# Wider contractions in the attention of an audio tower: 64 rows become 68 or 128, the added rows zero

## The chip, the cores and the metric

The kernel runs on one core of a Trainium2 chip, in one launch. The metric is the device time of that core in microseconds (us). The engines named below are TensorE (PE in the profile, its weight loads PEld), VectorE (DVE), ScalarE (ACT), GpSimd (POOL) and the queue engine SyncE (SP).

## The reference, cut to what matters

The input is x of shape (16, 750, 64). Three stages follow each other: a token stage (two dense layers, a square, two dense layers, a strided convolution that leaves 375 positions), a bidirectional recurrent stage over the 375 positions, and an attention whose keys and values are looked up with product keys. Only the last one is touched:

```
b, n, d = x.shape                                   # 16, 375, 64
q = (x @ Wq).reshape(b, n, HEADS, DIM) * DIM ** (-0.5)
kv_scores, indices = _pk(x, Wq_pk, pk_keys)         # 2 x top 16 of 64, then top 16 of the sums, softmax
ind = indices + offsets[None, None, :, None]
k = jnp.einsum('bnhk,bnhkd->bnhd', kv_scores, keys_table[ind])
v = jnp.einsum('bnhk,bnhkd->bnhd', kv_scores, values_table[ind])
sim = jnp.einsum('bihd,bjhd->bhij', q, k)
attn = jax.nn.softmax(jnp.where(causal, sim, neg), axis=-1)
out = jnp.einsum('bhij,bjhd->bhid', attn, v)
out = out.transpose(0, 2, 1, 3).reshape(b, n, HEADS * DIM)
return out @ Wo
```

There are 8 heads of 64 elements, so the scores, the queries, q times k, and v times Wo all contract over 64 elements.

## The kernel before, in words

The function `attention` works through 16 batches of 375 positions, cut in three pieces of 125. For heads 0 to 3 the table rows are gathered by GpSimd's indirect DMAs into `rows` and summed by TensorE with the weights `wmat` (the unit "eat"). For heads 4 to 7 the whole table of a head is multiplied: a batch has 64 steps (`STEPS`), and each step p has a fixed part on every engine.

- TensorE: `exponent` for step p+1 (products `ps<-parts,half`, and at each eighth step also `ps<-kdup,u`, which contract over 68 rows), `product` for step p-1 (`ps<-w,dtab`, 375 columns in 32 bits, contracting over 128 rows), `ranks` for step p+1 (`ps<-rank,half`, bf16), then the small units placed in this step.
- ScalarE: the exponential `ex` of the step, and copies out of PSUM for the units.
- VectorE: `weight`, which makes `w` from the rank sums and `ex`, then slices of the top-16 search for the next batch ("front").

Each product in 32 bits is two matmul records in the trace, each with its own weight load; the trace names it by weights and moving operand in alphabetical order.

The small units that contract over 64 rows are these, per batch: 24 `sim` (`ps<-kvT,qt`, q times k, 125 to 375 columns), 8 `value` (`ps<-cst,kvT`, three products of 64 columns each, v times Wo, on rows 64 to 127), 4 `query` (`ps<-u_dense,cst`), 8 `part` (`ps<-u_dense,kpart` or `ps<-u_front,kpart`), 3 `score` and 3 `score2` (`ps<-keymat,u_front`, 512 columns), and one opening of the output sum (in `weigh`, `ps<-cst` and `ps<-cst,h_now`). That is 51 units. Everything else that TensorE does in a batch contracts over 68, 125 or 128 rows.

In a step TensorE takes the units of bank 5, then of bank 6, then `weigh`, then the front's. `places()` puts the units into steps by fixed tables (`SIM_AT`, `PART_AT`, `VALUE_AT`, `QUERY_AT`) and a running sum of VectorE's time. By it part 0 of the next batch stands in step 49, and the unit "turn" that brings the max rows of the second piece into `u_front[64:68]` in step 44. Two of the 64-row units follow each other directly in five places per batch (steps 4, 11, 14, 25, 39), so a batch has 46 separate excursions to 64 rows. Before the first batch a prologue (`front` alone for 64 steps) does the search for batch 0; after the last one an epilogue finishes the last heads.

TensorE begins the attention with waits on the table `half`, which GpSimd's queue loads, and on the keys placed by VectorE.

Of the kernel before, what the change touches and what calls it, by code (L numbers as in the profile page):

```python
# [10 lines left out]
F32 = mybir.dt.float32  # L11
# [29 lines left out]
GH = 4  # L41
# [42 lines left out]
def build(nc, x, pack, early, halves, table, dense, minus, out):  # L84
    hu = nc.dram_tensor("rows_in", (2, B, D, T), F32).ap()
    with ExitStack() as ctx:
        cst = ctx.enter_context(nc.sbuf_tensor("cst", [128, WIDTH], F32))
        keymat = ctx.enter_context(nc.sbuf_tensor("keymat", [64, 1024], F32))
# [383 lines left out]
def turn_and_fold(nc, col, states, hist, keymat, ps):  # L472

    with nc.semaphore("b_key_product") as s_mm, nc.semaphore("b_copied") as s_cp, nc.Block() as block:
# [7 lines left out]
        @block.scalar  # L482
        def _(act):
            nc.scalar.copy(hist[0:64], states[:, :, 0:B]).then_inc(s_cp, 1)
            act.wait_ge(s_mm, 1)
            nc.scalar.copy(keymat[:].rearrange("p (k n) -> p k n", k=4), ps[0:64, 0:4, 0:256]).then_inc(s_cp, 1)
            act.wait_ge(s_cp, 3)
# [229 lines left out]
def attention(nc, cst, keymat, halves, table, dense, minus, hu, out, ps):  # L717
# [10 lines left out]
    with ExitStack() as ctx:  # L728
# [15 lines left out]
        kpart = sb("kpart", [64, DH, 2, 4, NK // 2])  # L744
# [7 lines left out]
        h_now = sb("h_now", [64, T])  # L752
# [25 lines left out]
        qt = sb("qt", [64, H, T])  # L778
# [11 lines left out]
        s_kdup = sem("d_keys_placed")  # L790
# [74 lines left out]
        def _(sp):  # L865
# [12 lines left out]
            def batch(n, kind):  # L878
                sp.wait_ge(s_cur, n + 1)
                sp.dma_start(h_now[:], hu[0, bass.ds(n, 1)].rearrange("o d t -> (o d) t")).then_inc(s_h, 16)  # L880
# [22 lines left out]
        def _(pool):  # L903
            pool.dma_start(half[:], halves[:]).then_inc(s_half, 16)
# [15 lines left out]
        def _(pe):  # L920
# [5 lines left out]
            pe.wait_ge(s_kdup, 16 + 4)  # L926

# [4 lines left out]
            def front(p, kind, b, f0):  # L932
                n = b - 1
                for which in range(2):
                    for key in here(which, p, kind):
                        name, c = key
                        f = f0 + c
                        if name == "score":
                            free(0, kind, n, key)
                            pe.wait_ge(s_row, b * 16 + 16)  # L940
                            mm(ps[0:TT, 5, :], u_front[0:64, c * TT:(c + 1) * TT], keymat[:, 0:512]).then_inc(s_fs, 1)
                        if name == "score2":
                            free(1, kind, n, key)
                            pe.wait_ge(s_row, b * 16 + 16)
                            mm(ps[0:TT, 6, :], u_front[0:64, c * TT:(c + 1) * TT], keymat[:, 512:1024]).then_inc(s_fs2, 1)
# [95 lines left out]

            def sim(m, kind, n):
# [3 lines left out]
                mm(ps[0:TT, 5, 0:(c + 1) * TT], qt[:, h, c * TT:(c + 1) * TT], kvT[0:64, h, 0:(c + 1) * TT]).then_inc(s_s, 1)  # L1046
# [9 lines left out]
            def weigh(m, kind, n):  # L1056
# [4 lines left out]
                if m == OLD:  # L1061
# [3 lines left out]
                    mm(ps[0:TT, 7, 0:NT * D], cst["causal"][0:64, 0:TT], cst["wq"][0:64, 0:NT * D], start=True, stop=False)  # L1065
# [587 lines left out]
```

## Time and profile before

| | us |
|---|---|
| median of 3 runs | 7148.5 |
| lowest and highest | 7143.23 and 7180.57 |
| the profiled execution | 7117.53 |
| its span | 7115.6 |

The profile is of one execution on the core. Its span covers the first to the last instruction, and 1.9 us lie around it. The profiled execution is 31 us (0.4%) below the median of the runs. The span has three parts: the token and recurrent stages (to 1027 us), the prologue of the attention (1027 to 1245 us), and its 16 batches with the epilogue (from 1245 us). A busy TensorE is not a TensorE at its peak: matmuls are pipelined and each record covers the way through the array too, so times between starts tell more than durations. TensorE's clock is granted at one of two levels, 1.2 and 2.4 GHz; a mean of 1.00 is 2.4 GHz throughout and 0.50 is 1.2 GHz throughout.

### The profile page before, as it was taken

Reading aid. Unit: us, or ns where it says so; the run is one execution under the profiler, and the core shown is the slowest. Engines: PE = TensorE matmul, PEld = TensorE weight load, DVE = VectorE, ACT = ScalarE, POOL = GpSimd, SP = SyncE. Lnnn points to the kernel's source line nnn. Section 1 sums busy time; section 2 is a strip of 40 time slices with the busy share of each in tenths; the row PEclk is TensorE's granted clock in tenths of the full one; section 3 lists DMA queues with packets and bytes.
Section 4 is the critical chain, followed back from the end, with each engine's and each line's share of the span. In section 5 each row is a group of like instructions: output and inputs, shape, how many; then the busy total and the mean of one; then the engine's idle time right before and its main releaser. Section 6 shows DMA issues by size and latency. Waiting matters only on the chain.

```text
span 7115.6 us, 93479 instructions
## 1 busy us (share of the span) xinstructions
PE 5480.1 (77%) x24308; PEld 3418.3 (48%) x24308; DVE 4305.4 (61%) x16637; ACT 2239.6 (31%) x5719; POOL 3127.9 (44%) x3404
## 2 busy tenths in 40 slices
PE   5666650778787888878888787878787888787889
PEld 4444420445454555545555454545445545454556
DVE  4666657666666565757566666665656575656522
ACT  4333320233332333333333232323333333333323
POOL 0011103555545455555554555554545555554541
PEclk8555575788787878888878787878787888888877
DMA  1000010122222222221222221212221222121220
GB/s 36 0 0 0 0 41 23 57 60 62 59 60 55 60 57 59 59 60 57 59 56 60 58 62 55 60 55 62 57 58 55 60 58 61 54 61 54 59 58 23
DMA packets 157826, 354.08 MB, mean 50 GB/s; under 512 B 71716, under 2 KB 75812, under 8 KB 156968
## 3 DMA queue, kind: packets, MB, share of 16 engines
q0 software_dynamic: 96912, 200.25, 10.6%
q1 hardware_dynamic: 60440, 148.26, 6.7%
q8 instruction: 207, 3.39, 0.2%
q14 instruction: 267, 2.19, 0.1%
HBM read 345.55 MB, written 4.61 MB: 49 GB/s over the span
## 4 chain that ended last, share of the span: by engine, by line
PE 33%; another core or an unknown queue 19%; DVE 16%; issue 12%; ACT 4%; DVEq 0%; DMA 0%; ACTq 0%; POOLq 0%
PE ps L922 33%; DVE topi L1317 2%; DVE w L1503 2%; DVE top L1311 2%; ACT ex L1180 1%; DVE sc L1323 1%; DVE idxf L1479 1%; DVE hot L1470 1%; DVE wmat L1495 1%; DVE eq L1440 1%; DVE cs L1323 1%; DVE eq L1448 1%; DVE left L1281 1%; DVE hot L1475 0%
## 5 line engine op out<-in xcount | busy, mean ns | idle before, releaser
L914 POOL DMA_INDIRECT rows<-table_dram,idxT x3024 | 3050.8, 1009 | 2898.8 <-PE ps L922 1603.7
L1503 DVE SCALAR_TENSOR_TENSOR w<-ps,ex 128x750 f32<-128x750 f32 x1024 | 960.1, 938 | 1918.4 <-remote 846.8
L922 PE MATMUL ps<-w,dtab 128*128 128x375 f32 x4096 | 1814.1, 573 | 11.1 <-issue 10.8
L922 PEld LDWEIGHTS ps<-w,dtab 128*128 128x128 f32 x4096 | 908.0, 229 | 481.3 <-issue 247.1
L1180 ACT ACTIVATE ex<-ps 128x750 f32<-128x750 f32 x1024 | 818.4, 799 | 710.8 <-PE ps L922 364.5
L922 PE MATMUL ps<-rank_dense,half 128*128 128x375 bf16 x1920 | 538.9, 367 | 485.8 <-DVE w L1503 360.7
L922 PEld LDWEIGHTS ps<-wmat,rows 128*128 128x128 f32 x6048 | 791.4, 208 | 137.6 <-issue 90.9
L922 PE MATMUL ps<-wmat,rows 128*128 128x8 f32 x6048 | 796.4, 266 | 54.9 <-issue 38.1
L922 PE MATMUL ps<-parts,half 128*128 128x375 bf16 x2048 | 605.3, 371 | 258.9 <-ACT ex L1180 183.6
L922 PEld LDWEIGHTS ps<-rank_dense,half 128*128 128x128 bf16 x1920 | 185.6, 108 | 999.0 <-DVE w L1503 525.6
L1194 ACT COPY kvg<-ps 128x28 f32<-128x28 f32 x432 | 79.6, 184 | 1418.7 <-remote 868.0
L361 PE MATMUL ps<-h_moving,early 128*64 128x32 f32 x2250 | 317.2, 297 | 242.1 <-DVE h_moving L454 242.1
L361 PEld LDWEIGHTS ps<-h_moving,early 128*64 128x64 f32 x2250 | 267.3, 219 | 433.7 <-DVE h_moving L454 433.6
L922 PE MATMUL ps<-dg,prob 125*125 125x125 f32 x1536 | 315.6, 338 | 194.6 <-ACT kvg L1195 109.3
L468 POOL COPY states<-n_h 64x32 f32 (+1 forms) x375 | 76.1, 203 | 849.5 <-DVE n_h L457 849.5
L922 PEld LDWEIGHTS ps<-parts,half 128*128 128x128 bf16 x2048 | 201.8, 117 | 420.0 <-ACT ex L1180 210.9
L922 PEld LDWEIGHTS ps<-dg,prob 125*125 125x125 f32 x1536 | 243.4, 226 | 316.6 <-issue 304.5
L1221 ACT COPY probT<-ps 125x125 f32<-125x125 f32 (+2 forms) x384 | 141.8, 369 | 620.6 <-PE ps L922 344.2
L1317 DVE FIND_INDEX8 topi<-top,sc 125x8 uint32<-125x64 f32 x1536 | 306.6, 224 | 45.3 <-issue 43.7
L922 PE MATMUL ps<-kvT,qt 64*125 64x125 f32 (+2 forms) x768 | 292.4, 464 | 34.7 <-ACT vout L1204 13.2
L922 PE MATMUL ps<-vout,probT 125*125 125x64 f32 x1536 | 284.5, 316 | 29.4 <-issue 19.5
L922 PEld LDWEIGHTS ps<-vout,probT 125*125 125x125 f32 x1536 | 239.4, 222 | 88.0 <-issue 65.5
(207 smaller groups left out, 6968.9 us busy)
## 6 DMA issues: line engine op xcount, KB each, us to landing
dtab<-dense_dram SPq DMA_DIRECT2D x256, 512.0 KB
rows<-table_dram,idxT POOLq DMA_INDIRECT x3024
xin<-x_dram SPq DMA_DIRECT2D x16, 187.5 KB
half<-halves_dram POOLq DMA_DIRECT2D x1, 1828.0 KB, 13.1
early<-early_dram SPq DMA_DIRECT2D x1, 1800.5 KB, 9.6
rows_in<-hh SPq DMA_DIRECT2D x16, 93.8 KB, 2.2
rows_in<-uu SPq DMA_DIRECT2D x16, 93.8 KB, 2.2
u_front<-rows_in SPq DMA_DIRECT2D x16, 93.8 KB
```

The lines of the kernel that those rows point to most:

```text
L361: return nc.tensor.matmul(out_, lhsT, rhs, start=start, stop=True, skip_group_check=True)
L468: nc.gpsimd.tensor_copy(states[:, bass.ds(s, 1), :].rearrange("p o b -> p (o b)"), after[:, k, 1::2]).then_inc(s_kept, 1)
L914: nc.gpsimd.indirect_dma_start(out=rows[:, t, :], out_offset=None, in_=table[:, :], in_offset=bass.IndirectOffsetOnAxis(ap=idxT[:, c, t:t ...
L922: return nc.tensor.matmul(out_, lhsT, rhs, start=start, stop=stop, skip_group_check=open_bank)
L1180: nc.scalar.activation(ex[:, p % 2, :, :], ps[:, 0:2, 0:T], ACT.Exp).then_inc(s_ex, 1)
L1194: nc.scalar.copy(kvg[:, :, c * TT + t0:c * TT + t1], src[:, 0])
L1221: nc.scalar.copy(probT[:, m % 2, 0:J], ps[0:TT, 6, 0:J]).then_inc(s_empty[1], 1)
L1281: nc.vector.tensor_tensor(left[64:128, half, :], ps[64:128, 5 + half, 0:T], parts[64:128, h % 2, half, :], ALU.subtract).then_inc(s_empty[ ...
L1311: last = nc.vector.max(best[:, g, 8 * half:8 * half + 8], values[:, g, :])
L1317: last = nc.vector.max_index(where[:, g, 8 * half:8 * half + 8], best[:, g, 8 * half:8 * half + 8], values[:, g, :])
L1323: last = nc.vector.match_replace(values[:, g, :], best[:, g, 8 * half:8 * half + 8], values[:, g, :], LOWEST)
L1503: nc.vector.scalar_tensor_tensor(w[:, p % 2, :, :], ps[:, 2:4, 0:T], float(K), ex[:, p % 2, :, :], ALU.is_gt, ALU.mult).then_inc(s_w, 1)
```

## The change

Tiles that met 64-row products get more partitions, and the products take them all. `keymat` and `kpart` get 68 partitions, `h_now` and `qt` 128. The added rows are zero. Where the other operand has numbers in these rows (the max rows of `u_front`, the value half of `kvT`), they meet the zeros. Scores, parts and queries now contract over 68 rows; sim, value and the opening over 128. GpSimd zeroes the added rows once at the start of the attention, TensorE waits for that once, and part 0 waits for the max rows of the pieces that are written by then.

```diff
-        kpart = sb("kpart", [64, DH, 2, 4, NK // 2])
+        kpart = sb("kpart", [68, DH, 2, 4, NK // 2])
-        h_now = sb("h_now", [64, T])
+        h_now = sb("h_now", [128, T])
-        qt = sb("qt", [64, H, T])
+        qt = sb("qt", [128, H, T])
...
         def _(pool):
+            for blank in (u_front[64:68], keymat[64:68], kpart[64:68], h_now[64:128], qt[64:128]):
+                nc.gpsimd.memset(blank, 0.0).then_inc(s_blank, 1)
             pool.dma_start(half[:], halves[:]).then_inc(s_half, 16)
...
             pe.wait_ge(s_kdup, 16 + 4)
+            pe.wait_ge(s_blank, 5)
...
-                            mm(ps[0:TT, 5, :], u_front[0:64, c * TT:(c + 1) * TT], keymat[:, 0:512]).then_inc(s_fs, 1)
+                            mm(ps[0:TT, 5, :], u_front[:, c * TT:(c + 1) * TT], keymat[:, 0:512]).then_inc(s_fs, 1)
...
                 if h == 0:
                     pe.wait_ge(s_row, n * 16 + 32)
+                    pe.wait_ge(s_um, n * NT + NT + 2)
...
-                mm(ps[:, 5 + half, 0:T], kpart[:, h, half].rearrange("p a k -> p (a k)"), u[0:64, :]).then_inc(s_pt, 1)
+                mm(ps[:, 5 + half, 0:T], kpart[:, h, half].rearrange("p a k -> p (a k)"), u[:, :]).then_inc(s_pt, 1)
...
-                mm(ps[:, 5, 0:T], cst["wq"][0:64, h * D:(h + 2) * D], u_dense[0:64, :]).then_inc(s_aq, 1)
+                mm(ps[:, 5, 0:T], cst["wq"][0:68, h * D:(h + 2) * D], u_dense[:, :]).then_inc(s_aq, 1)
...
-                    last = mm(ps[0:TT, 5, c * D:(c + 1) * D], kvT[64:128, h, c * TT:(c + 1) * TT],
-                              cst["wo"][64:128, h * D:(h + 1) * D])
+                    last = mm(ps[0:TT, 5, c * D:(c + 1) * D], kvT[:, h, c * TT:(c + 1) * TT],
+                              cst["wo"][:, h * D:(h + 1) * D])
...
-                mm(ps[0:TT, 5, 0:(c + 1) * TT], qt[:, h, c * TT:(c + 1) * TT], kvT[0:64, h, 0:(c + 1) * TT]).then_inc(s_s, 1)
+                mm(ps[0:TT, 5, 0:(c + 1) * TT], qt[:, h, c * TT:(c + 1) * TT], kvT[:, h, 0:(c + 1) * TT]).then_inc(s_s, 1)
...
-                    mm(ps[0:TT, 7, 0:NT * D], cst["causal"][0:64, 0:TT], cst["wq"][0:64, 0:NT * D], start=True, stop=False)
+                    mm(ps[0:TT, 7, 0:NT * D], cst["causal"][:, 0:TT], cst["wq"][:, 0:NT * D], start=True, stop=False)
...
-                nc.scalar.mul(qt[:, h, :], ps[0:64, 5, 0:T], -(D ** -0.5))
+                nc.scalar.mul(qt[0:64, h, :], ps[0:64, 5, 0:T], -(D ** -0.5))
```

`score2` and the residual's products change like `score`; VectorE's, ScalarE's and SyncE's writes into the widened tiles are limited to their old rows, with the same columns. No instruction of TensorE, ScalarE, VectorE or SyncE changes its place. On GpSimd, at the entry to the attention, the queue read before (L902 is the entry, `half` the table of bf16 constants):

```order
L902 UNCONDITIONAL_BRANCH [waits barrier_Pool_Activation_PE_DVE_SP_gather]
L904 DMA half<-halves_dram 128x7312
L905 UNCONDITIONAL_BRANCH
L905 ISA
L911 ISA [waits c_turned_copied]
```

and reads now:

```order
L902 UNCONDITIONAL_BRANCH [waits barrier_Pool_Activation_PE_DVE_SP_gather]
L905 MEMSET u_front 4x375
L905 MEMSET keymat 4x1024
L905 MEMSET kpart 4x1024
L905 MEMSET h_now 64x375
L905 MEMSET qt 64x3000
L906 DMA half<-halves_dram 128x7312
```

So five memsets of 5798 columns in all stand ahead of the load of `half`. On TensorE, part 0 and part 1 of the next batch (`kpart` is the part's key table) read before, and now:

```order
L922 MATMUL ps<-u_front,kpart 128x375 [waits c_rows_loaded,c_bank5_emptied]
L922 MATMUL ps<-u_front,kpart 128x375 [waits c_rows_loaded,c_bank6_emptied]
```

```order
L924 MATMUL ps<-u_front,kpart 128x375 [waits c_max_rows_copied,c_rows_loaded,c_bank5_emptied]
L924 MATMUL ps<-u_front,kpart 128x375 [waits c_max_rows_copied,c_rows_loaded,c_bank6_emptied]
```

The one wait on the max rows is what was added there; nothing moved.

## Rows read from the trace of the kernel before

**Rows 1.** The page's part 1: busy us, share of the span, instructions.
```profile
PE 5480.1 (77%) x24308; PEld 3418.3 (48%) x24308; DVE 4305.4 (61%) x16637; ACT 2239.6 (31%) x5719; POOL 3127.9 (44%) x3404
```
**Rows 2.** Busy time by stretch: three stages; columns as in the head.
```profile
core 0: us, PE busy (x) PEld busy (x) DVE busy (x) ACT busy (x) POOL busy (x), PEclk, DMA share, GB/s
0.00:1027.00 1027.00, 690.64 (x3332) 412.40 (x3332) 602.70 (x2438) 338.52 (x1270) 76.31 (x379) 0.59 0.03 9
1027.00:1245.50 218.50, 22.74 (x73) 10.45 (x74) 158.30 (x743) 17.06 (x29) 66.46 (x64) 0.50 0.14 38
1245.50:7071.00 5825.50, 4727.54 (x20773) 2965.97 (x20773) 3538.91 (x13429) 1869.52 (x4375) 2985.09 (x2961) 0.82 0.20 58
```
**Rows 3.** The chain of waits from 1300 to 7050 us, shares by line.
```profile
by line: PE ps L922 39.9%; another core or an unknown queue 23.4%; issue 14.6%; DVE w L1503 2.8%; DVE topi L1317 2.6%; DVE top L1311 1.6%; ACT ex L1180 1.6%; DVE sc L1323 1.0%; DVE wmat L1495 0.7%; DVE idxf L1479 0.7%; DVE left L1281 0.7%; 
```
**Rows 4.** Waits from 1245.5 us on: who, for whom, us, times, longest.
```profile
ACT kvg L1194 <- remote: 868.0, 173, 12.7
PE ps L922 <- DVE w L1503: 361.1, 170, 22.2
```
**Rows 5.** Timeline of PE: a 64-row sim between others, clock 1.00; start, us.
```profile
3010.76 0.49 PE L922 MATMUL ps<-rank_dense,half 128*128 128x375 bf16 x2 [1.51 <-DVE w L1503]
3011.19 0.89 PE L922 MATMUL ps<-kvT,qt 64*125 64x375 f32 x2
3012.01 0.48 PE L922 MATMUL ps<-dg,prob 125*125 125x125 f32 x2
3012.33 0.48 PE L922 MATMUL ps<-parts,half 128*128 128x375 bf16 x2
```
**Rows 6.** The same of a 68-row product of the same columns, clock 1.00.
```profile
3006.88 0.33 PE L922 MATMUL ps<-parts,half 128*128 128x375 bf16 x1
3007.04 0.79 PE L922 MATMUL ps<-u_dense,kdup 68*128 68x375 f32 x2
3007.67 0.32 PE L922 MATMUL ps<-parts,half 128*128 128x375 bf16 x1
```
**Rows 7.** Timeline of PEld: the weight loads of the two.
```profile
3006.88 0.35 PEld L922 LDWEIGHTS ps<-u_dense,kdup 68*128 68x128 f32 x2 [0.22 <-issue]
3011.19 0.29 PEld L922 LDWEIGHTS ps<-kvT,qt 64*125 64x125 f32 x2 [0.31 <-issue]
3012.01 0.29 PEld L922 LDWEIGHTS ps<-dg,prob 125*125 125x125 f32 x2 [0.53 <-issue]
```
**Rows 8.** Timeline of PE at clock 0.50: both kinds again.
```profile
2602.58 1.46 PE L922 MATMUL ps<-u_dense,kdup 68*128 68x375 f32 x2
2603.82 0.52 PE L922 MATMUL ps<-parts,half 128*128 128x375 bf16 x1
...
2800.00 0.83 PE L922 MATMUL ps<-rank_dense,half 128*128 128x375 bf16 x2
2800.77 1.61 PE L922 MATMUL ps<-kvT,qt 64*125 64x375 f32 x2
2802.31 0.78 PE L922 MATMUL ps<-dg,prob 125*125 125x125 f32 x2
2802.88 0.52 PE L922 MATMUL ps<-parts,half 128*128 128x375 bf16 x1
```
**Rows 9.** Timeline of all engines at the start of the attention.
```profile
1027.75 0.73 POOL L904 DMA_DIRECT2D half<-halves_dram  x1 [101.63 <-POOLq L498]
...
1040.92 3.77 PE L922 MATMUL ps<-keymat,u_front 64*125 64x512 f32 x4 [21.25 <-DMA half<-halves_dram]
```
**Rows 10.** Groups by form: a memset of VectorE, a copy of GpSimd; mean ns.
```profile
L252 DVE MEMSET steps<- 64x6000 f32 x1 | 5.1, 5058 | 2.1 <-issue 2.1
...
L468 POOL COPY states<-n_h 64x32 f32 x360 | 73.1, 203 | 822.9 <-DVE n_h L457 822.9
```
**Rows 11.** Busy time by stretch around a fall of the clock at 1774.5 us.
```profile
1764.00:1774.40 10.40, 10.40 (x73) 8.30 (x72) 9.53 (x27) 3.95 (x12) 3.78 (x4) 1.00 0.23 72
1774.60:1777.80 3.20, 3.20 (x7) 1.25 (x7) 1.90 (x2) 0.41 (x3) 2.59 (x3) 0.50 0.16 41
```

More of the change, by code:

```diff
@@ L87, in build @@
         cst = ctx.enter_context(nc.sbuf_tensor("cst", [128, WIDTH], F32))
-        keymat = ctx.enter_context(nc.sbuf_tensor("keymat", [64, 1024], F32))
+        keymat = ctx.enter_context(nc.sbuf_tensor("keymat", [68, 1024], F32))
         ps = ctx.enter_context(nc.psum_tensor("ps", [128, 8, 512], F32))
@@ L485, in _ @@
             act.wait_ge(s_mm, 1)
-            nc.scalar.copy(keymat[:].rearrange("p (k n) -> p k n", k=4), ps[0:64, 0:4, 0:256]).then_inc(s_cp, 1)
+            nc.scalar.copy(keymat[0:64].rearrange("p (k n) -> p k n", k=4), ps[0:64, 0:4, 0:256]).then_inc(s_cp, 1)
             act.wait_ge(s_cp, 3)
@@ L789, in attention @@
         s_pt, s_hi, s_mid, s_lo = (sem(n) for n in ("d_part_product", "d_part_high", "d_part_middle", "d_part_low"))
-        s_kdup = sem("d_keys_placed")
+        s_kdup, s_blank = sem("d_keys_placed"), sem("c_unused_rows_zeroed")
         s_half, s_passed = sem("c_halves_loaded"), sem("c_passed")
@@ L879, in batch @@
                 sp.wait_ge(s_cur, n + 1)
-                sp.dma_start(h_now[:], hu[0, bass.ds(n, 1)].rearrange("o d t -> (o d) t")).then_inc(s_h, 16)
+                sp.dma_start(h_now[0:64], hu[0, bass.ds(n, 1)].rearrange("o d t -> (o d) t")).then_inc(s_h, 16)
                 if kind != "last":
@@ L944, in front @@
                             pe.wait_ge(s_row, b * 16 + 16)
-                            mm(ps[0:TT, 6, :], u_front[0:64, c * TT:(c + 1) * TT], keymat[:, 512:1024]).then_inc(s_fs2, 1)
+                            mm(ps[0:TT, 6, :], u_front[:, c * TT:(c + 1) * TT], keymat[:, 512:1024]).then_inc(s_fs2, 1)
                         if name == "part" and c < 2:
@@ L1064, in weigh @@
                         pe.wait_ge(s_osb, n)
-                    mm(ps[0:TT, 7, 0:NT * D], cst["causal"][0:64, 0:TT], cst["wq"][0:64, 0:NT * D], start=True, stop=False)
+                    mm(ps[0:TT, 7, 0:NT * D], cst["causal"][:, 0:TT], cst["wq"][:, 0:NT * D], start=True, stop=False)
                     for j in range(NT):
-                        mm(ps[0:TT, 7, j * D:(j + 1) * D], h_now[:, j * TT:(j + 1) * TT], ident[0:64, 0:D], start=False, stop=False)
+                        mm(ps[0:TT, 7, j * D:(j + 1) * D], h_now[:, j * TT:(j + 1) * TT], ident[:, 0:D], start=False, stop=False)
                 for j in range(c + 1):
@@ L1198, in query @@
                 act.wait_ge(s_aq, n * (H // 2) + (query_order[h] + 1))
-                nc.scalar.mul(qt[:, h, :], ps[0:64, 5, 0:T], -(D ** -0.5))
-                nc.scalar.mul(qt[:, h + 1, :], ps[64:128, 5, 0:T], -(D ** -0.5)).then_inc(s_empty[0], 1)
+                nc.scalar.mul(qt[0:64, h, :], ps[0:64, 5, 0:T], -(D ** -0.5))
+                nc.scalar.mul(qt[0:64, h + 1, :], ps[64:128, 5, 0:T], -(D ** -0.5)).then_inc(s_empty[0], 1)
             def value(h, n):
@@ L1263, in _ @@
             nc.vector.memset(mz[:], 0.0)
-            nc.vector.memset(kpart[:, :, :, 1, :], 0.0).then_inc(s_kdup, 1)
-            side0 = keymat[:, GH * NK:H * NK].rearrange("p (h k) -> p h k", h=DH)
-            side1 = keymat[:, (H + GH) * NK:2 * H * NK].rearrange("p (h s k) -> p h s k", h=DH, s=2)
+            nc.vector.memset(kpart[0:64, :, :, 1, :], 0.0).then_inc(s_kdup, 1)
+            side0 = keymat[0:64, GH * NK:H * NK].rearrange("p (h k) -> p h k", h=DH)
+            side1 = keymat[0:64, (H + GH) * NK:2 * H * NK].rearrange("p (h s k) -> p h s k", h=DH, s=2)
             nc.vector.tensor_copy(kdup[0:64], side0.unsqueeze(2).broadcast_to([64, DH, 2, NK])).then_inc(s_kdup, 1)
-            nc.vector.tensor_copy(kpart[:, :, :, 0, :], side1).then_inc(s_kdup, 1)
-            nc.vector.tensor_copy(kpart[:, :, :, 2, :], side1)
-            nc.vector.tensor_copy(kpart[:, :, :, 3, :], side1).then_inc(s_kdup, 1)
+            nc.vector.tensor_copy(kpart[0:64, :, :, 0, :], side1).then_inc(s_kdup, 1)
+            nc.vector.tensor_copy(kpart[0:64, :, :, 2, :], side1)
+            nc.vector.tensor_copy(kpart[0:64, :, :, 3, :], side1).then_inc(s_kdup, 1)
             dve.wait_ge(s_half, 16)
```

## The prediction

> **What bounds the kernel now.** I read the busy shares first, then the stretches, then the chain, then single products. TensorE is the busiest engine, 77% of the span against 61% of VectorE [rows 1]. The stretches show where: before 1027 us nothing of this change runs; in the prologue TensorE is busy for 23 of 218 us and VectorE for 158; from 1245.5 us TensorE is busy for 4728 of 5825 us, VectorE for 3539 [rows 2]. So the change earns in the last stretch or nowhere.
>
> There neither engine is busy all the time, so I take the chain [rows 3]. The reader is to see 39.9% on TensorE's line and 23.4% put down to an unknown releaser. The second is mostly TensorE too: the largest such wait is ScalarE's for the gathered sums, 868 us, and those come from TensorE alone [rows 4]. Together 63% of the stretch lies on TensorE. The rest is on VectorE, ScalarE and their issue, and there TensorE waits (361 us for `w` alone, with one wait of 22 us [rows 4]). I use 0.63 as the share of TensorE's savings that reaches the end. It is a share of time, not a slope: near enough for a saving of a few per cent, too high if the other engines take over soon.
>
> **What a 64-row product costs.** Starts of neighbours tell it. At full clock two bf16 products take 0.32 us, but the sim behind them starts 0.43 us after the first: 0.11 lost at the entry [rows 5]. The sim, two records of 375 columns, holds TensorE for 0.82 us until dg starts [rows 5]; a product of the same columns over 68 rows holds it for 0.63 [rows 6]. That is 0.19 more. The two dg records behind it take 0.32 us [rows 5], and I estimate 0.22 for them where the array is not left, since 375-column records run at 0.16 in bf16 and 0.31 in 32 bits, and 125 columns in 32 bits cannot stream longer than a third of 0.31, with a load of about 0.1 between starts: 0.10 more. In sum 0.40 us. The loads show how: behind the 64-row sim the next load starts 0.53 us after the last one ended, behind the 68-row product 0.22 us after [rows 7]. The load before and behind a 64-row product is not taken ahead; over 68 rows it is. So what decides is 64 against more, and 68 is enough. At half clock the same three steps are 0.77 against 0.64 (two bf16 records of 0.32), 1.54 against 1.24, and 0.57 against some 0.42: 0.13, 0.30 and 0.15, in sum 0.58 us [rows 8].
>
> Where bf16 products follow, the last term is near nothing, and a value's columns are few: 0.30 us at full clock. I take 0.36 at full clock and 0.55 at half. The mean clock 0.82 [rows 2] means 36% of the time at 1.2 GHz, but TensorE idles more there, so I weight 84 to 16: 0.39 us. The ends are 0.30 and 0.58.
>
> The Trainium skill (TensorE: Matmul & The Clock Gate, Part 2) says that weight loads are pulled ahead of running matmuls when the row groups do not conflict or when the background weight buffer is the target. By row groups alone a load over all rows could never go ahead, and the wider products would gain nothing; by the buffer they gain in full. The 68-row product between full-height ones, whose neighbours' loads go ahead, speaks for the buffer.
>
> **The sum, part by part.**
> - The pauses: 46 excursions in each of 16 batches are 736, times 0.39 us is 287 us of TensorE's time. Times 0.63 it is 181 us off the end. The ends for this term: 736 x 0.58 = 427 us all on the chain, and zero.
> - The wider rows themselves: nothing. Time goes by columns, and those stay: the 68-row load and the 128-row records of [rows 5, 6] run at the columns' pace.
> - The clock. TensorE spent 36% of the stretch at 1.2 GHz, where a product takes twice as long (0.31 against 0.62 for a 32-bit record of 375 columns [rows 6, 8]). What did it do before the clock fell? At 1774.5 us it had been busy for 10.40 of 10.40 us by its records [rows 11], so busy records alone do not hold the clock; much of that stretch is small products. The change puts streaming in the place of pauses in 287 of 5825 us, 5% of the stretch, and puts more rows into each product. I estimate that 4% of the stretch changes from 1.2 to 2.4 GHz. One per cent is 58 us, half of that is saved if TensorE is on the chain, times 0.63 is 18 us. So 73 us; ends: 14 points in the wrong direction (below) and 10 points in the right one, 183 us. This is the softest term. The Trainium skill (the same page, Part 1) has the clock follow how busy the array has been, with no word on rows; by that only the 5% count, not the rows.
> - GpSimd's memsets: 5798 columns ahead of the load of `half`, for which TensorE waits 21 us and which starts GpSimd's queue [rows 9]. Nothing hides them: VectorE and TensorE both wait for `half`. VectorE zeroes 6000 columns in 5.06 us, 0.84 ns a column, which gives 4.9 us; GpSimd's copy of 32 columns in 203 ns gives 6.3 ns a column, 37 us, most of it surely a fixed cost [rows 10]. The operation is nearest to the first: I take 6 us, ends 5 and 37.
> - The added waits. TensorE's wait for the memsets ends before that for `half`, which is queued behind them: nothing. Part 0's wait for the max rows: the last copy it needs belongs to "turn" in step 44, and part 0 stands in step 49, so five steps of some 5.7 us (5825 us over 1024 steps) lie between: nothing. If that cover were gone, the parts, exponents and products behind it would wait too, and with them `w`. In the prologue it may cost a copy of half a microsecond once, beside a VectorE that is busy anyway.
> - Epilogue and prologue: in the prologue VectorE is the bound, nothing is gained. The last 45 us at half clock have some 15 sims in a chain: at 0.5 us some 7 us, inside my rounding.
>
> Against the profiled execution: 7117.5 - 181 - 73 + 6 = 6869.5 us. The median of the runs is 31 us above it, so the forecast is 6900 us.
>
> **The rivals.** "Same" means within 0.5% of 7148.5, or 36 us, about what a measurement of this kernel can tell from no change.
>
> 1. *The others take over.* VectorE's search slices and its stalls stay, and TensorE only reaches its wait for `w` earlier. For it: TensorE waits 361 us for `w` already, and VectorE's 3539 us are 61% of the stretch. Against it: VectorE itself idles for 39% of it. Priced at a third of the 287 us and no clock gain: 7117.5 - 96 + 6 + 31 = 7059 us.
> 2. *More than expected.* The units lie in the steps that are bound by TensorE, so the whole 287 us count, and the clock gains 10 points: 7117.5 - 287 - 183 + 6 + 31 = 6685 us. For it: the steps with most units are the long ones. Against it: the chain's 37% elsewhere.
> 3. *It doesn't do what it says.* The pause belongs to something other than the 64 rows, say to the unit's own operands, and stays. Against it: [rows 7]. Then the memsets alone remain: 7148.5 + 6 = 7155, up to 7186 us with 37.
> 4. *The clock falls more often: slower.* TensorE now finishes its units sooner and waits longer for `w` in the steps that VectorE bounds; a TensorE that waits loses its clock, and every product behind it takes double. From 36% to 50% of the stretch at 1.2 GHz is 14 points, 252 us: 7148.5 - 181 + 252 + 6 = 7226 us. It decides from 12 points on, (181 + 36) over 18. For it: the 22 us wait. Against it: the total of waits grows less than the work becomes denser.
>
> **Chances.** The forecast (6810 to 6990) 0.62, the first rival (to 7100) 0.20, the second 0.08, the third 0.05, the fourth 0.05. Faster by over 0.5%: 0.62 + 0.20 + 0.08, less a hundredth of the first that ends near no change, 0.89. Same: the third and that hundredth, 0.06. Slower: 0.05. The range runs from 6770 to 7070 us: it holds the forecast, most of the first rival and a piece of the second.
>
> **What would show it.** If the steps are right, the sims have 125*128 or 128-row forms, the load behind a sim comes 0.2 us after the last one and not 0.5, and the time from a sim's start to the next product is 0.63 us for 375 columns. TensorE's idle time behind `w` grows by about a third of 287 us. The mean clock of the batches is 0.83 to 0.86; at 0.82 the clock term was nothing, below 0.79 the fourth rival speaks. The load of `half` starts about 6 us later behind the entry. The forecast is wrong if the pauses stay at 0.5 us, or if they go and the stretch from the first exponent to the end still takes over 5720 us.

## The result and the profile after

The changed kernel took 7122.0 us (median of 17 runs, 7091 to 7152) beside 7152.8 us of the kernel before (median of 17, 7122 to 7199): ratio 0.9959, 95% interval [0.9939, 0.9978]. That is 31 us, 0.4%. Forecast were 6900 us, range 6770 to 7070. The profiled run of the changed kernel took 7139 us, span 7137.1.

First the page's part 1, then the busy times of the three stages (columns as in [rows 2]). They answer to [rows 1, 2]. The last line is the same work as 1245.5 to 7071 us before: from the first exponent, which now starts 4.4 us later, to 45 us before the end.

```profile
PE 5195.9 (73%) x24308; PEld 3406.4 (48%) x24308; DVE 4307.0 (60%) x16637; ACT 2249.5 (32%) x5719; POOL 3116.9 (44%) x3409
```
```profile
0.00:1027.00 1027.00, 691.22 (x3332) 412.54 (x3332) 602.71 (x2438) 339.00 (x1270) 76.33 (x379) 0.59 0.03 9
1027.00:1250.00 223.00, 22.61 (x74) 10.64 (x74) 162.49 (x743) 17.16 (x29) 71.49 (x69) 0.50 0.14 37
1245.50:7071.00 5825.50, 4426.40 (x20599) 2941.09 (x20600) 3528.69 (x13406) 1862.93 (x4334) 2969.08 (x2961) 0.82 0.20 58
1249.90:7092.10 5842.20, 4446.69 (x20718) 2956.21 (x20719) 3532.84 (x13412) 1872.34 (x4354) 2969.08 (x2961) 0.83 0.20 58
```

Over the same work TensorE is busy for 4447 us instead of 4728, 281 us less (284 over the whole program, 5480 to 5196), and the stretch is no shorter: 5842 us in this execution beside 5825 in the one profiled before. TensorE's idle time in it grew from 1098 to 1396 us. The mean clock of the stretch rose a little, from 0.82 to 0.83; over whole executions it is 0.779 to 0.787 in the 17 runs of the changed kernel and 0.765 to 0.776 in the 68 runs of the kernel before in the jobs of e1 to e16. Singly, the products did what was forecast. The timeline of PE at full clock, answering to [rows 5]:

```profile
2762.66 0.79 PE L924 MATMUL ps<-kvT,qt 128*125 128x375 f32 x2
2763.29 0.38 PE L924 MATMUL ps<-dg,prob 125*125 125x125 f32 x2
2763.50 0.80 PE L924 MATMUL ps<-u_dense,kdup 68*128 68x375 f32 x2
```

The 375-column sim holds TensorE for 0.63 us (0.82 before), `dg` for 0.21 (0.32 before). The loads (PEld, answering to [rows 7]; this sim has 125 columns) show no pause ahead of the sim:

```profile
2982.52 0.10 PEld L924 LDWEIGHTS ps<-rank_dense,half 128*128 128x128 bf16 x1 [0.22 <-issue]
2982.68 0.35 PEld L924 LDWEIGHTS ps<-kvT,qt 128*125 128x125 f32 x2
```

So the saving was made and came back as idle time of TensorE. The chain of waits from 1300 to 7050 us (answers to [rows 3]), then the waits from 1245.5 us on (answer to [rows 4]):

```profile
by line: PE ps L924 29.7%; another core or an unknown queue 28.6%; issue 15.4%; DVE w L1507 3.3%; DVE topi L1321 2.8%; DVE top L1315 2.0%; ACT ex L1184 1.8%; DVE sc L1327 1.1%; DVE hot L1474 1.0%; DVE idxf L1483 0.9%; DVE cs L1327 0.9%; DVE
```
```profile
ACT kvg L1198 <- remote: 836.7, 169, 11.2
DVE w L1507 <- remote: 833.0, 110, 20.2
...
PE ps L924 <- DVE w L1507: 415.7, 239, 18.3
```

TensorE's line falls from 39.9% to 29.7% of the chain. The unknown releaser ("remote" in the waits) rises from 23.4% to 28.6%. The kernel runs on one core, so no other core is behind it. In the kernel before, VectorE's `w` waits 847 us for it. All such waits of all engines but SyncE, each over 0.15 us, sum to 3126 us before and 3353 us after from 1245.5 us on; TensorE itself has only 15 and 55 us of them. One such place, in the timeline of the kernel before (columns: start, us, engine, line, operation, then the idle time before it and its releaser):

```profile
3919.88 0.83 PE L922 MATMUL ps<-rank_dense,half 128*128 128x375 bf16 x2
...
3926.36 0.80 ACT L1180 ACTIVATE ex<-ps 128x750 f32<-128x750 f32 x1 [6.94 <-issue]
...
3935.20 0.94 POOL L914 DMA_INDIRECT rows<-table_dram,idxT  x1 [0.31 <-issue]
...
3939.70 0.94 DVE L1503 SCALAR_TENSOR_TENSOR w<-ps,ex 128x750 f32<-128x750 f32 x1 [19.63 <-remote]
```

`w` needs the rank products, ended at 3920.7 us by the records, and the exponentials `ex`, ended at 3927.16. It starts at 3939.70, 12.5 us after the later of the two. VectorE had been free since 3920.08, and TensorE was busy for 5.5 of the 19 us. GpSimd issues gathers one behind another until 3936.1. I call this a **late start**: the time from the latest of three ends (rank products, exponentials, the engine's own previous instruction) to the start of `w`, and the like for `ex`, which needs the `parts` products. Only those over 0.5 us count. Summed over the 1024 steps they are 844 us before (549 for `w`, 295 for `ex`) and 881 us after (532 and 350).

Last, the start of the attention in the changed kernel (answers to [rows 9]):

```profile
1028.36 4.78 DVE L1271 COPY kdup<-keymat 64x512 f32<-64x512 f32 x1
...
1030.26 2.59 POOL L905 MEMSET qt<- 64x3000 f32 x1
1032.81 0.72 POOL L906 DMA_DIRECT2D half<-halves_dram  x1
...
1046.11 3.78 PE L924 MATMUL ps<-keymat,u_front 68*125 68x512 f32 x4 [25.88 <-DMA half<-halves_dram]
```

TensorE starts 5.2 us later than before, 4.6 if one counts from VectorE's first instruction of the stage (1027.49 before, 1028.05 here).

### The profile page after: what moved, and what is told of

It is laid out like the page before. It is cut to its first block, busy times and chain, and to the rows that moved or that the text cites. A ratio compares the mean times of both kernels' runs of the same rounds, so it can differ in the third digit from the quotient of the medians.

```text
span 7137.1 us, 93499 instructions
## 1 busy us (share of the span) xinstructions
PE 5195.9 (73%) x24308; PEld 3406.4 (48%) x24308; DVE 4307.0 (60%) x16637; ACT 2249.5 (32%) x5719; POOL 3116.9 (44%) x3409
## 4 chain that ended last, share of the span: by engine, by line
PE 25%; another core or an unknown queue 23%; DVE 19%; issue 13%; ACT 4%; DVEq 0%; DMA 0%; ACTq 0%; POOL 0%; POOLq 0%
PE ps L924 25%; DVE w L1507 3%; DVE topi L1321 3%; DVE top L1315 2%; ACT ex L1184 1%; DVE sc L1327 1%; DVE hot L1474 1%; DVE idxf L1483 1%; DVE cs L1327 1%; DVE eq L1452 1%; DVE eq L1444 1%; DVE left L1285 1%; DVE wmat L1499 1%; DVE fin L1315 1%
## 5 line engine op out<-in xcount | busy, mean ns | idle before, releaser
L924 PE MATMUL ps<-w,dtab 128*128 128x375 f32 x4096 | 1753.2, 557 | 40.2 <-issue 40.2
L924 PEld LDWEIGHTS ps<-w,dtab 128*128 128x128 f32 x4096 | 885.7, 224 | 496.8 <-issue 253.1
L924 PE MATMUL ps<-wmat,rows 128*128 128x8 f32 x6048 | 780.0, 264 | 63.2 <-issue 43.3
L924 PE MATMUL ps<-dg,prob 125*125 125x125 f32 x1536 | 293.0, 321 | 195.1 <-DVE wmat L1499 92.9
L924 PE MATMUL ps<-kvT,qt 128*125 128x125 f32 (+2 forms) x768 | 265.0, 430 | 97.6 <-ACT vout L1208 45.8
L924 PE MATMUL ps<-vout,probT 125*125 125x64 f32 x1536 | 258.6, 296 | 30.5 <-issue 21.5
```

The costliest lines, as they stand in the source:

```text
L924: return nc.tensor.matmul(out_, lhsT, rhs, start=start, stop=stop, skip_group_check=open_bank)
```

## The experiments

Two theories at the start. A: stretches in which GpSimd gathers bound both kernels, through the late starts. B: VectorE takes over as the bound. The expectations also weigh a third, C: TensorE is the bound at its real pace.

**e1 and e2: one gather in seven**, in the kernel before and in the changed one.

```diff
-                        for t in GROUPS[g]:
+                        for t in GROUPS[g][:1]:
...
+            nc.vector.memset(rows[:], 0.0).then_inc(s_rz, 1)
```

> The kernel before with one indirect DMA per group of gathered rows in place of seven (6 of 7 rows of heads 0 to 3 are left zero; TensorE's products stay). Theory A (the stretches in which VectorE and ScalarE wait long past TensorE's recorded end, some 840 us in the trace of before, go with GpSimd's long gather bursts): at least 400 us faster than before. Theory B (VectorE's own work is what bounds the batches, the first rival of the prediction): within 60 us of before. Theory C (TensorE is the bound at its real pace): within 60 us too.

> The changed kernel with the same cut of the gathers. Theory A: faster than the same cut of before by 100 to 250 us, since the waits that swallowed TensorE's savings are gone. Theory B: by no more than 50 us, as with the gathers. Theory C: by about 180 us with and without gathers, which the whole kernel has not shown.

Measured: 5644.5 us, ratio 0.7875 [0.7857, 0.7892], and 5530.0 us, ratio 0.7721 [0.7705, 0.7738]. The late starts are zero in both. B and C, each as the only cause, had e1 within 60 us of the kernel before, and fall with this. The unknown releaser is gone too: no wait of any engine is put down to it. Here the change is worth 114 us, 2.0%. Windows from the first exponent to 45 us before the end of each (columns as in [rows 2]), what TensorE waits for, and the chain of e1 from 1300 to 5580 us:

```profile
1211.60:5600.60 4389.00, 4182.29 (x20773) 2704.46 (x20773) 3510.54 (x13428) 1887.97 (x4374) 465.41 (x423) 0.93 0.12 39
```
```profile
1217.40:5483.40 4266.00, 3930.49 (x20713) 2737.29 (x20714) 3492.26 (x13411) 1885.23 (x4354) 463.25 (x423) 0.94 0.13 40
```
```profile
PE ps L923 <- DVE w L1506: 149.9, 159, 2.9
```
```profile
PE ps L925 <- DVE w L1510: 277.8, 224, 2.9
```
```profile
by line: PE ps L923 60.2%; issue 11.6%; DVE w L1506 3.7%; DVE topi L1320 3.7%; DVE top L1314 2.4%; DVE eq L1443 1.8%; DVE sc L1326 1.6%; DVE eq L1451 1.4%; DVE hot L1473 1.4%; DVE idxf L1482 1.3%; DVE left L1284 1.3%; DVE wmat L1498 1.0%; D
```

In the first two kinds, the first line is e1 and the second e2. TensorE's busy time falls by 252 us, its wait for `w` rises by 128, and the stretch is 123 us shorter. Even without late starts, then, 114 of 252 us reach the end, 0.45. The rest becomes a wait for VectorE. And 1.5 ms of the kernel go with the gathers, against 0.3 ms of saved TensorE time. Of the 1.44 ms by which e1's long stretch is shorter than before, 0.89 ms are idle time of TensorE (1098 to 207 us) and 0.55 ms its busy time (4728 to 4182 us) under a mean clock of 0.93 instead of 0.82. So the gathers cost clock as well as waiting.

**e3 and e4: less work on VectorE**, both kernels. Its three operations on `hot` go over 2 candidates instead of 50, so the indices of the gathered rows are wrong.

```diff
-  hot[:], posf[...].broadcast_to([TT, 2, K, CAND])
+  hot[:, :, :, 0:2], posf[...].broadcast_to([TT, 2, K, 2])
```

> The kernel before with the three long operations that turn positions into table rows cut from 50 columns to 2 (6 slices of 1.82 us for each piece become short; some wrong rows are fetched, as many as before). That takes 6 x 1.7 x 48 = 490 us of VectorE's busy time. Theory B: at least 200 us faster. Theories A and C: less than 80 us faster.

> The changed kernel with the same cut on VectorE. Theory B: faster than the same cut of before by 100 us or more, since VectorE no longer takes over. Theory A: by the same 30 us as uncut, give or take 30.

Measured: 7139.3 us, 0.9961 [0.9937, 0.9986], and 7040.1 us, 0.9834 [0.9788, 0.9880]. Late starts 750 and 755 us. Theory B alone falls: the kernel before gives back 26 us for 460 us of VectorE's work (three groups of 96 at 1.82 us become 0.22). Theory A alone falls too: between e3 and e4 the change is worth 99 us, where A had it at 30 give or take 30, although the late starts are as long in e4 as in e3. So the work of VectorE holds back the saving in the whole kernel as well: 99 of the 278 us that TensorE's busy time falls here (4682 to 4404 us) reach the end, 0.36. One thing blurs each of the two by itself: the wrong rows keep the DMA engines busy for 0.62 of the stretch instead of 0.20, in e3 and e4 alike.

**e5 and e6: all gathers, nobody waits for them.** They land in a tile that nothing reads.

```diff
-                                out=rows[:, t, :], out_offset=None, in_=table[:, :],
+                                out=aside[:, t % (3 * GROUP), :], out_offset=None, in_=table[:, :],
...
-                pe.wait_ge(s_g[g], n * (NT * share) + (c + 1) * share)
```

> The kernel before, with all 3024 gathers kept on GpSimd, at the same points of the program, but landing in a tile that nothing reads; TensorE multiplies a tile of zeros in their place and no longer waits for gathered rows. So the attention over the gathered heads is left out and the output is not the reference's; the instructions of all engines but for a few waits are those of before. The run with one gather in seven took 5644 us against 7165, and there the late starts of VectorE's weights and ScalarE's exponentials (0.8 ms in sum) were gone. Theory 1 (the wait for the gathered rows holds the in-order TensorE back, and the rest follows from that wait): 5650 to 5800 us, late starts under 0.1 ms. Theory 2 (the issuing of gathers itself delays what TensorE signals to the other engines, whoever needs the rows): 6900 to 7150 us, late starts still 0.6 ms or more.

> The changed kernel with the same edit: all gathers kept, landing in a tile that nothing reads, TensorE not waiting for them (the attention over the gathered heads is left out). Theory 1 (the wait for the rows): 5530 to 5700 us, some 110 us under the same edit of before. Theory 2 (the issuing itself): 6880 to 7120 us, within 60 us of the same edit of before, late starts 0.6 ms or more.

Measured: 7149.2 us, 1.0015 [0.9993, 1.0036], and 7120.8 us, 0.9976 [0.9953, 0.9999]; late starts 773 and 784 us. The wait for the data is nothing; the late starts and the time come with the issuing. The row of VectorE's waits in e5 still has the unknown releaser:

```profile
DVE w L1512 <- remote: 702.0, 83, 17.5
```

**e7: plain loads by GpSimd** in the place of six gathers in seven.

```diff
-                        for t in GROUPS[g]:
+                        for t in GROUPS[g][1:]:
+                            pool.dma_start(rows[:, t, :], table[t * 128:(t + 1) * 128, :]).then_inc(s_g[g], 16)
+                        for t in GROUPS[g][:1]:
```

> The kernel before, with six of the seven gathers of each group replaced by plain loads of the same size (64 KB into 128 rows) issued by GpSimd on the same queue; TensorE waits for them as for gathers. The rows loaded are not the ones asked for, so the output is not the reference's. If the addressing by indices is the cost (1.25 us from one gather to the next in a burst), plain loads are issued faster and the time falls below 6500 us; if any load of 64 KB that GpSimd issues costs the same, the time stays at 7100 to 7200 us and the late starts stay at 0.8 ms.

Measured: 5641.4 us, 0.7901 [0.7880, 0.7923], no late starts. 

**e8: the same bytes by SyncE**, ten plain loads of 64 KB behind each piece, beside one gather in seven.

```diff
+                    for j in range(10):
+                        sp.dma_start(aside[:, j, :], table[(i * 10 + j) * 64:(i * 10 + j) * 64 + 128, :]).then_inc(s_aside, 16)
```

> The kernel before with one gather in seven (5644 us), and in addition 2560 plain loads of 64 KB each, ten behind each of the 256 loads of a piece of the table, issued by SyncE on its own queue into a tile that nothing reads. The DMA engines so move about as many bytes as before, in rows of 512 B too, with GpSimd nearly idle. The sums over the gathered heads lack six rows in seven, so the output is not the reference's. If the traffic of the DMA engines makes the late starts and the long time: 6800 to 7200 us and late starts of 0.5 ms or more. If it is GpSimd's issuing: 5640 to 5800 us and late starts under 0.1 ms; the loads of pieces may be some microseconds later behind the extra ones.

Measured: 5622.3 us, 0.7886 [0.7856, 0.7915], no late starts, with 352 MB moved (354 before). So neither the traffic nor GpSimd's plain loads do it, only its gathers by index.

**e9: the memsets behind the load of `half`** in the changed kernel.

```diff
-            for blank in (u_front[64:68], keymat[64:68], kpart[64:68], h_now[64:128], qt[64:128]):
-                nc.gpsimd.memset(blank, 0.0).then_inc(s_blank, 1)
             pool.dma_start(half[:], halves[:]).then_inc(s_half, 16)
+            for blank in (u_front[64:68], keymat[64:68], kpart[64:68], h_now[64:128], qt[64:128]):
+                nc.gpsimd.memset(blank, 0.0).then_inc(s_blank, 1)
```

> The changed kernel, complete, with one edit: GpSimd issues the load of `half` first and zeroes the unused rows behind it. The memsets took from 1027.78 to 1032.85 us ahead of that load and TensorE started 5.2 us later than before. Expected: TensorE starts at 1041 us again, 5 us less than the changed kernel in all (some 7117 us beside a before of 7150), ratio to before 0.995; 0.9959 with no effect is not excluded by the interval. If the memsets slowed nothing but the load of `half`, nothing else changes.

Measured: 7132.6 us, 0.9990 [0.9962, 1.0019]. TensorE starts at 1040.57 us, 13.5 us behind VectorE's first instruction as in the kernel before (18.1 in the changed one), and nothing of that is seen at the end: the expected ratio was 0.995, and this kernel is as fast as the one before, so the 0.4% of the change is not seen in this job.

**e10 and e11: a wait behind each gather**, with a memset of 1 and of 500 columns, on top of e9.

```diff
                             ).then_inc(s_g[g], 16)
+                            nc.gpsimd.memset(pause[:], 0.0).then_inc(s_pause, 1)
+                            pool.wait_ge(s_pause, n * (NT * PAIR_ROWS) + (c * PAIR_ROWS + t + 1))
```

> The kernel of e9 with a pause of GpSimd behind each gather: a memset of one column (some 0.1 us) and a wait for it, so that gathers in a burst start some 1.5 us apart and not 1.25. Complete computation. If a back-to-back series of gathers is what holds TensorE's signals back, the late starts fall from 0.88 ms to under 0.4 ms and the time below 6900 us. If each gather has a price whatever stands between two (0.58 us each by e1), the time stays at 7100 to 7150 us. If GpSimd's rate bounds the kernel, it becomes slower: 3024 times 0.25 us is 756 us, up to 7800 us.

> As e10 with a memset of 500 columns (0.43 us by the rate of 64x3000 in 2.59 us), so that gathers start some 1.9 us apart: 63 of them take 120 us, which is all the time that a slice has (364 us a batch, three slices). If spacing is what matters: late starts under 0.2 ms and below 6700 us, as long as GpSimd keeps up. If each gather has its price: 7100 us or more. If GpSimd's rate bounds: 3024 x 0.65 us on top of bursts that fill 65% of the stretch, some 7300 to 8000 us.

Measured: 7271.9 us, 1.0197 [1.0159, 1.0236], and 8528.8 us, 1.1956 [1.1911, 1.2001]. The late starts are zero in both, beside a kernel before of 7131 us on the same chip. In their place TensorE waits for rows. Timeline of GpSimd and the wait in e10:

```profile
3003.08 0.11 POOL L922 MEMSET pause<- 128x1 f32 x1
3004.00 0.95 POOL L918 DMA_INDIRECT rows<-table_dram,idxT  x1 [0.81 <-POOL pause L922]
```
```profile
PE ps L929 <- DMA rows<-table_dram,idxT: 1230.7, 253, 10.5
```

A gather every 1.87 us cures the late starts and is too slow itself: 189 times 1.87 us is 353 us, nearly the whole batch of 364. I had expected 1.5 us between gathers in e10; the wait costs more than the memset. In e11 they come 2.29 us apart instead of the expected 1.9, and the time lies above the expected range (to 8000 us).

**e12: gathers and plain loads in turn**, four gathers and three plain loads in a group, in the kernel before.

```diff
+                            if t % GROUP % 2 == 1:
+                                pool.dma_start(rows[:, t, :], table[t * 128:(t + 1) * 128, :]).then_inc(s_g[g], 16)
+                                continue
```

> The kernel before with three of the seven gathers of a group replaced by plain loads of the same size by GpSimd, so that gathers and plain loads alternate (the rows of the plain loads are not the ones asked for, so the output is not the reference's). 1728 gathers remain of 3024; none remain with six plain in seven but 432, at 5641 us against 7138. If each gather has a fixed price, the time lies on the line between: 5641 + 1296 x 0.58 = 6390 us, and late starts 0.35 to 0.5 ms. If only a series without gaps does it: 5650 to 5900 us, late starts near nothing.

Measured: 5635.2 us, 0.7908 [0.7874, 0.7942], no late starts. With 1728 gathers left it is as fast as with 432: the price is not a fixed one for each gather. Its timeline of GpSimd:

```profile
3023.64 0.97 POOL L917 DMA_INDIRECT rows<-table_dram,idxT  x1 [0.30 <-issue]
3024.61 0.60 POOL L915 DMA_DIRECT2D rows<-table_dram  x1
3025.51 0.97 POOL L917 DMA_INDIRECT rows<-table_dram,idxT  x1 [0.30 <-issue]
3026.49 0.60 POOL L915 DMA_DIRECT2D rows<-table_dram  x1
3027.39 0.97 POOL L917 DMA_INDIRECT rows<-table_dram,idxT  x1 [0.30 <-issue]
3028.67 0.95 POOL L917 DMA_INDIRECT rows<-table_dram,idxT  x1 [0.30 <-issue]
```

Two gathers with a plain load between them start 1.88 us apart, two next to each other 1.28. A group of seven has three of the first distance and one of the second, so in the mean a gather comes every 1.7 us here, and no faster elsewhere.

**e13 to e16: a memset without a wait**, behind each group of seven (e13 before, e14 changed) or each gather (e15 before, e16 changed).

```diff
+                            nc.gpsimd.memset(pause[:, c * PAIR_ROWS + t:c * PAIR_ROWS + t + 1], 0.0).then_inc(s_pause, 1)
```

> The kernel before, complete, with one addition: behind each group of seven gathers GpSimd zeroes one column of a small tile (0.11 us by e10), with a wait for them once a batch. In e10 and e12, where no more than one or two gathers stood directly behind each other, the late starts were zero; in the kernel before they are 0.84 ms in 63 gathers behind each other. Theory 2a (a long unbroken series of gathers does it, and any other GpSimd work resets it): late starts under 0.1 ms, 5650 to 5900 us (the floor of e1, e7 and e12 is 5640; GpSimd needs 27 x 9.0 = 243 us of a batch of 266). Theory 2b (already a few gathers behind each other do it): 6400 us or more, late starts 0.4 ms or more.

> The changed kernel, complete, with the same addition. By theory 2a 100 to 120 us under the same edit of before (as e2 under e1: 114 us), 5540 to 5790 us; by theory 2b within 60 us of the same edit of before.

> The kernel before, complete, with one column zeroed by GpSimd behind every gather, without a wait but once a batch. e10 had this with a wait behind each (gathers 1.9 us apart, GpSimd the bound, 7272 us, no late starts). Here gathers come some 1.35 to 1.45 us apart: 189 of them take 255 to 275 us, about a batch of the kernel without late starts (266 us). Expected if the break alone matters: no late starts, 5700 to 6000 us, TensorE waiting for gathered rows for 50 to 300 us. If GpSimd's memset costs more than that between gathers (0.6 us as in e10): 7000 us or more.

> The changed kernel, complete, with the same addition behind every gather. Where GpSimd's rate bounds, TensorE's saving cannot reach the end: 0 to 60 us under the same edit of before. Where it does not bound: 100 to 120 us under.

Measured: 7128.1 us, 0.9992 [0.9967, 1.0018]; 7160.5, 1.0038 [1.0021, 1.0056]; 7232.0, 1.0102 [1.0062, 1.0143]; 7229.9, 1.0125 [1.0104, 1.0146]. Late starts 888, 910, 898 and 919 us. Theory 2a as I put it falls: other work of GpSimd between gathers resets nothing. For e15 I had expected 5700 to 6000 us or 7000 and more, with gathers 1.35 to 1.45 us apart. The timeline of e15 shows why it could not tell more; the gathers stay 1.25 us apart:

```profile
3001.30 0.94 POOL L916 DMA_INDIRECT rows<-table_dram,idxT  x1 [0.19 <-issue]
3002.23 0.12 POOL L920 MEMSET pause<- 128x1 f32 x1
3002.54 0.94 POOL L916 DMA_INDIRECT rows<-table_dram,idxT  x1 [0.19 <-issue]
```

These four also show what 0.4% means here. With the memset behind each group the changed kernel is 32 us slower than the one before; without it, 31 us faster; with one behind each gather, 2 us. A memset behind each gather also makes the kernel before 99 us slower, though the gathers come as fast as ever. So the sign of the change hangs on details beside it. That it is how the steps fall against the gathers is a guess; no run varied that alone.

**e17 and e18: a wait behind every third gather**, the changed kernel, one kernel in two jobs.

```diff
+                            if t % 3 == 2:
+                                nc.gpsimd.memset(pause[:], 0.0).then_inc(s_pause, 1)
+                                pool.wait_ge(s_pause, n * (NT * 21) + (c * 21 + t // 3 + 1))
```

> The changed kernel, complete; behind every third gather GpSimd zeroes one column and waits for that before it goes on (e10 had this behind every gather: gathers 1.87 us apart, no late starts, GpSimd the bound at 7272 us; e15 and e16 had the memset without the wait: gathers still 1.25 us apart, late starts unchanged). Gathers so come 1.25, 1.25 and 1.87 us apart, 1.46 us in the mean; 189 of them take 276 us of a batch. If the rate of gathers is what decides and 1.46 us is slow enough (e12 had 1.7 us and more between gathers in the mean): no late starts and 5750 to 6050 us, with GpSimd as the bound or near it. If every stretch without a wait of more than one or two gathers does it: late starts still over 0.3 ms, 6900 to 7250 us.

> The kernel of e17 once more, in a job of its own. In e17 the kernel before, run beside it, took 5626 us, where it took 7131 to 7165 us in all other jobs; so e17 says nothing on whether the wait behind every third gather removes the late starts, since nothing shows that they were there. If the kernel before takes some 7140 us beside this run: 5916 us and no late starts if the mean rate of 1.46 us a gather, or the gap in every third, is enough (ratio 0.83); over 6900 us and late starts over 0.3 ms if it is not. If the kernel before takes 5626 us again, the ratio is 1.05 again and the question stays open.

Measured: 5915.8 us, 1.0509 [1.0489, 1.0529], and 5906.2 us, 1.0489 [1.0466, 1.0511]. In these two jobs, each on a chip not used by the others, the kernel before itself took 5626 and 5633 us (medians of 7), where it took 7131 to 7165 on the four chips of the jobs before, and 7149 and 7153 in the two measurements ahead of these. So what the gathers cost differs by chip, or by something that goes with the job, by 1.5 ms: 5630 us is also what e1, e7, e8 and e12 reach on the others with fewer gathers (5622 to 5645). The mean clock of whole executions says the same: 0.853 to 0.858 in the 14 runs of the kernel before here, 0.852 to 0.859 in those four, 0.765 to 0.776 in the kernel before elsewhere. The changed kernel itself was not run on these two chips. By e1 and e2 it would gain about 2% there, which is an estimate. The chain of e17 from 1300 to 5850 us shows GpSimd as the bound, as expected of 1.46 us a gather:

```profile
by line: POOL rows L918 49.5%; issue 31.9%; PE ps L930 8.0%; POOL pause L923 2.1%; DVE w L1513 1.2%; DMA rows<-table_dram,idxT 1.1%; DVE topi L1327 1.0%; DVE top L1321 0.5%; POOLq L864 0.4%; DVE cs L1333 0.3%; DVE eq L1450 0.3%; DVE left L1
```

Whether it would take 5910 us where the kernel before takes 7140 was not seen: neither job fell there. No complete version was measured to beat both kernels.

## Why the prediction was wrong

- **The pauses** (736 times 0.39, 287 us of TensorE's time): right in kind, somewhat high in size. The steps of the sim and of `dg` came to 0.63 and 0.21 us, as worked out. TensorE's busy time fell by 281 us, but this holds what the clock gave too (3123 to 3028 us at 2.4 GHz, 1604 to 1418 at 1.2 GHz). At the old mix of the two levels it would be some 226 us, 0.31 us for each excursion; this is an estimate from these four numbers. The rule weighed there, of the Trainium skill (TensorE: Matmul & The Clock Gate, Part 2), by which a load goes ahead into the background buffer, agrees with the loads shown above: no pause over 0.22 us.
- **Their share that reaches the end, 0.63**: this step failed. Measured are 31 of 281 us, 0.11. The share came from the chain, in two parts. I read the 23.4% of the unknown releaser as "mostly TensorE too", from the row of `kvg`. The row beside it, 847 us of `w` for the same releaser, I did not look at. Both rows lose that releaser in e1 (`kvg` then waits 751 us, for TensorE by name), in a kernel that is 1.5 ms faster. Much of that time is late starts, and they did not get shorter with TensorE's products: 844 us before, 881 after. The other part is that a share of time is no slope, even in a clean chain: e1's has 60.2% on TensorE and nothing unknown, and 0.45 of the saving reaches the end.
- **What the runs show in its place** are two things together. Without late starts 0.45 of the saving arrives (e1 to e2). With the late starts as they are and 460 us less work on VectorE, 0.36 (e3 to e4). With both in place, 0.11. No run takes away both, and how they join, so that so little arrives, stays open.
- **The clock term, 73 us** (116 us of TensorE's time before the share of 0.63): too large. The mean clock over the same work went from 0.817 to 0.826, so 1.7% of the stretch changed its level and not 4%; that is the other 55 of the 281 us. TensorE's saved time became idle time, and its busy share of the stretch fell from 81% to 76%. In e1 and e2, where it is idle for 5% and 8% of the stretch, the clock of the long stretch is 0.93 and 0.94.
- **The memsets, 6 us**: 4.6 to 5.2 us later at the start. In the whole kernel they are lost in the spread of the runs (e9). In the profiles of e1 and e2 the stretch from the first exponent on is 123 us shorter and the whole execution 117, so there about 6 us do reach the end.
- **The wider rows and the added waits, nothing**: nothing seen against it.
- **The first rival** (7059 us: the others take over, a third of the saving arrives) had the right direction, and e3 and e4 bear out its mechanism. Its size was too small, since it too left the late starts out. The third and fourth did not happen: the pauses went, and the clock did not fall. The bound that I had set (the stretch from the first exponent to the end still over 5720 us) was passed: it is some 5887 us.
- **What I missed** in the profile of before: [rows 2] has GpSimd busy for half of the stretch and VectorE for 61%, TensorE for 81%, none full. The step from there was to ask who releases the long waits. Single late starts stood in the timeline, 14 of the 15 longest of `w` at the same two steps of a batch, 25 and 36.

What is **shown**, on the four chips of e1 to e16: the late starts come with gathers by index on GpSimd that follow each other every 1.25 us; neither anybody's need of their data, nor the bytes moved, nor GpSimd's plain loads make them; with 1.7 us and more between gathers in the mean they are gone, in e12 with a plain load in most gaps, in e10 and e11 with a wait of GpSimd in each. Whether it is the rate or what fills the gaps is not separated. Also shown is that on two chips the kernel before takes 5630 us. What is **argued** only: that the kernel before has no late starts on those chips (its time and its clock fit, there is no trace of it), and that TensorE's signals are what comes late. In the place shown, ScalarE, VectorE and SyncE are all released late by waits for TensorE, and by the records its products had ended; a late signal and a late last write look the same there. Why indexed gathers at that rate would do it stays open.

## What to carry to other kernels

A chain of waits with a quarter of its time on an unknown releaser has no known slope: look at the longest of those waits one by one, at what its inputs' records say and at what else runs there, before a share of time is taken as the share of a saving that arrives. When two causes may hold a saving back, take each away in both kernels: here either one gave back about 100 us. Compare windows that hold the same work, not the same microseconds. A change of 0.4% in such a kernel is of the size of small details: memsets of one column turned its sign. And one job, one chip: before a cost is held to be the kernel's, see it on a second chip.

## What the runs showed of the hardware

- Gathers by index by GpSimd (128 rows of 512 B each) 1.25 us apart cost 1.5 ms of 7.1 on four chips, and nothing that can be seen on two others. Each has a record of 0.94 us; a plain load of the same size has 0.56 to 0.60, and with six plain loads in seven (e7) the kernel takes 5641 us.
- A memset of one column between two gathers leaves their pace at 1.25 us (0.12 us within the 0.30 between their records), but with one behind each gather the kernel before takes 7232 us beside 7133 (e15). A wait for it makes 1.25 us into 1.87.
- A 64-row product among full-height ones cost TensorE some 0.3 us (the estimate above, 226 us in 736 excursions), and 0.40 us around a sim of 375 columns at full clock [rows 5, 6]. With 68 or 128 rows the pauses are gone.
- VectorE's copy of `kdup` took 4.78 us beside GpSimd's memsets; with the load of `half` ahead of them it took 0.35, and a copy of 64x256 behind it, which then lay beside them, took 5.26 instead of 0.27. The Trainium skill (SBUF — State Buffer, SBUF: two separate sides) has VectorE, in its two-port modes, and GpSimd share a pair of ports as an exclusive lock, under which the later one waits. The trace agrees: the copy ends at 1033.14 us and the last of the five memsets at 1032.85. That this copy ran in such a mode is not shown.
